# Fourier stage: widenings, filter products and returned blocks one part sooner; scan: SiLU block ahead of the decay of step 5

## What is computed

```python
x = x + _L0_conv_ref(_gn(x), ...)   # 3x3 neighbours weighted by a score
x = x + _L1_conv_ref(_gn(x), ...)   # two selective-scan (mamba) layers over the pixels
x = x + _L2_conv_ref(_gn(x), ...)   # Fourier filter on 8x8 patches, 3x3 conv, gated GELU
x = x + _L3_conv_ref(_gn(x), ...)   # cosine transform of 8x8 blocks, rounded
```

```python
dA = exp(delta * A); dBu = delta * B * u
h = dA[t] * h + dBu[t];  y[t] = sum_n h * C[t];  y = (y + u * D) * silu(res)
```

```python
x = einsum(x, w_in)                       # 64 -> 384 channels
x = irfft2(rfft2(8x8 patches of x) * fft_filter)
x = depthwise 3x3 conv of x;  x1, x2 = split(x)
return einsum(gelu(x1) * x2, w_out)       # 192 -> 64 channels
```

## Time and profile before

| | us |
|---|---|
| median of 3 runs | 19109.42 |
| lowest, highest | 19099.32, 19221.73 |
| the profiled execution, its own time | 19099.55 |
| its span, first to last instruction | 19097.7 |
| VectorE busy | 17998.3 (94%) |
| GpSimd busy | 17116.8 (90%) |
| TensorE busy | 13183.2 (69%) |
| ScalarE busy | 11214.6 (59%) |

### The profile page before, as it was taken

The page is one execution under the profiler, slowest core; times in us unless marked ns, Lnnn a source line. Parts: engine busy times, 40 slices in busy tenths (PEclk is TensorE's granted clock), DMA queues, the critical chain, the costliest instruction groups (busy, mean ns, idle before and its releaser), DMA issues. The chain is left out here.

```text
span 19097.7 us, 148278 instructions
## 1 busy us (share of the span) xinstructions
PE 13183.2 (69%) x46046; PEld 4686.6 (25%) x46046; DVE 17998.3 (94%) x11644; ACT 11214.6 (59%) x12335; POOL 17116.8 (90%) x7353
## 2 busy tenths in 40 slices
PE   4876666666666666666666666666666669999985
PEld 2321111111111111111111111111111134444444
DVE  5989999999999999999999999999999979999996
ACT  1116666666666666666666666666666646666663
POOL 3989999999999999999999999999999969999991
PEclk8997777777777777777777777777777779999997
DMA  4335555555555555555555555555555511111114
GB/s 125 114 109 138 134 135 139 139 134 138 139 134 136 140 138 133 137 139 137 134 139 139 134 137 140 137 133 138 139 138 134 137 49 34 34 34 34 34 29 146
DMA packets 616199, 2249.26 MB, mean 118 GB/s; under 512 B 74881, under 2 KB 92147, under 8 KB 591091
## 3 DMA queue, kind: packets, MB, share of 16 engines
q1 hardware_dynamic: 610146, 2232.63, 45.1%
q10 hardware_dynamic: 5265, 7.14, 0.1%
HBM read 990.77 MB, written 174.96 MB: 61 GB/s over the span
## 5 line engine op out<-in xcount | busy, mean ns | idle before, releaser
L1324 POOL TENSOR_TENSOR h<-h,c_bc 128x1024 f32<-128x1024 f32 x4096 | 9603.5, 2357 | 789.4 <-DVE h L1280 742.6
L1280 DVE TENSOR_TENSOR_SCAN h<-da,state,px 128x1024 f32<-128x1024 f32 x3072 | 7209.3, 2347 | 109.6
L1151 ACT ACTIVATE da<-d_bc,a_neg 128x1024 f32<-128x1024 f32 x3072 | 3492.6, 1144 | 2643.9 <-DVE h L1280 2619.4
L1005 PE MATMUL py<-h,ysel 128*32 128x512 f32 x16384 | 2740.3, 801 | 2587.8 <-POOL h L1324 2587.3
L1274 DVE TENSOR_TENSOR px<-px,du_bc 128x1024 f32<-128x1024 f32 x3072 | 3782.8, 1231 | 312.0 <-PE px L991 86.9
L1926 POOL TENSOR_TENSOR acc<-acc,ta 128x1024 f32<-128x1024 f32 (+1 forms) x976 | 2273.0, 2339 | 230.3 <-DVE acc L1826 135.8
L1316 POOL TENSOR_TENSOR xs<-du_bc,b_bc 128x1024 f32<-128x1024 f32 x1024 | 2409.6, 2353 | 0.0
L1280 DVE TENSOR_TENSOR_SCAN h<-px,state,xs 128x1024 f32<-128x1024 f32 x1024 | 2316.8, 2326 | 0.0
L1826 DVE SCALAR_TENSOR_TENSOR p_c<-zb,w_dw,p_c 128x1024 f32<-128x1024 f32 (+1 forms) x1560 | 1983.2, 1271 | 135.7 <-PE p_c L1591 112.2
L991 PE MATMUL px<-cf,bsel 32*128 32x512 f32 x3072 | 1339.8, 959 | 916.5 <-DVE h L1280 916.5
L1151 ACT ACTIVATE px<-d_bc,a_neg 128x1024 f32<-128x1024 f32 x1024 | 1144.6, 1118 | 900.6 <-DVE h L1280 885.9
(11 more groups left out here) (219 smaller groups left out, 19460.0 us busy)
## 6 DMA issues: line engine op xcount, KB each, us to landing
d_bc<-delta SPq DMA_DIRECT2D x1024, 512.0 KB, 8.5
du_bc<-du SPq DMA_DIRECT2D x1024, 512.0 KB, 8.5
c_bc<-c_rows_dram SPq DMA_DIRECT2D x1024, 512.0 KB, 5.3
b_bc<-c_rows_dram SPq DMA_DIRECT2D x256, 512.0 KB, 8.1
hx<-x_dram SPq DMA_DIRECT2D x252, 256.5 KB, 6.3
st_x<-in_x_dram SPq DMA_DIRECT2D x32, 1024.0 KB, 4.9
ax<-in_x_dram SPq DMA_DIRECT2D x64, 512.0 KB, 3.4
xr<-x_dram SPq DMA_DIRECT2D x64, 512.0 KB, 6.1
```

The source lines that it names most:

```text
L1005: last = nc.tensor.matmul(py[32 * j:32 * j + 32, cut], ysel[:, :], h[:, (4 * q + j) % 8, cut], start=False, stop=(q == Q - 1))
L1151: nc.scalar.activation(out[:, :], d_bc[:, n % J, :], ACT.Exp, scale=a_neg[t.l][:, n:n + 1]).then_inc(da_done, 1)
L1280: nc.vector.tensor_tensor_scan(h[:, n % 8, PAD:T + PAD], a[:, :], x[:, :], state[:, 2 * t.l + t.b, n:n + 1], ALU.mult, ALU.add).then_inc(s ...
L1324: nc.gpsimd.tensor_tensor(out=h[:, n % 8, 0:T], in0=h[:, n % 8, PAD:T + PAD], in1=c_bc[q % 2][:, :], op=ALU.mult).then_inc(m2_done, 1)
```

## The change

In the scan, ScalarE's `main` has the SiLU block of the task `after` ahead of decay 5 instead of behind it. In the Fourier stage the tables change: widening p moves from tick 3p + 1 to 3p, filter p from ahead of tap 3p + 3 to ahead of tap 3p + 2, the back-transforms by one tick; with them the pieces of unit 1 and one of unit 3 come a tick later, the next slot's first conv, the first projection, the third transpose and frequency step and GELU a tick sooner, and ScalarE's taps move by up to four ticks. No instruction is added or removed.

```diff
--- before.py
+++ after.py
@@ -1163,9 +1163,9 @@
                 decay(t, 4)
                 if before:
                     keep_state(before, 3)
-                decay(t, 5)
                 if after:
                     front_silu(after)
+                decay(t, 5)
                 decay(t, 6)
                 decay(t, 7)
                 if after:
@@ -1463,20 +1463,20 @@
         LOW, HIGH = slice(0, 64), slice(64, 128)
 
         TICKS = 6 * ND
-        CONV_AT = {0: (1, 0), 1: (1, 1), 5: (2, 0), 6: (2, 1), 7: (2, 2), 8: (2, 3), 10: (3, 0), 11: (3, 1),
+        CONV_AT = {1: (1, 0), 2: (1, 1), 5: (2, 0), 6: (2, 1), 7: (2, 2), 8: (2, 3), 10: (3, 0), 12: (3, 1),
                    15: (4, 0), 16: (4, 1), 17: (4, 2), 18: (4, 3), 20: (5, 0), 21: (5, 1), 22: (5, 2), 23: (5, 3)}
-        NEXT_AT = 27
-        PROJECT_AT = (4, 9)
-        WIDEN_AT = {3 * p + 1: p for p in range(NP)}
-        BACK_AT = {3 * (j // 2) + 4 + j % 2: j for j in range(NJ)}
+        NEXT_AT = 26
+        PROJECT_AT = (3, 9)
+        WIDEN_AT = {3 * p: p for p in range(NP)}
+        BACK_AT = {3 * (j // 2) + 3 + j % 2: j for j in range(NJ)}
 
         FIRST = 3
-        TURN_AT = ({13: 0, 19: 1, 25: 2}, {13: 3})
-        FREQ_AT = ({17: 0, 22: 1, 26: 2}, {16: 3})
-        TAP_AT = {2: (0, 0), 3: (0, 1), 4: (0, 2), 5: (1, 0), 6: (1, 1), 7: (1, 2), 9: (2, 0), 10: (2, 1), 14: (3, 0), 16: (3, 1),
-                  18: (3, 2), 21: (4, 0), 22: (4, 1), 26: (5, 0), 27: (5, 1)}
-        CARRY_AT, GELU_BACK_AT, GELU_AT = 1, (11, 12), (23, 24)
-        FILTER_N = {3 * p + 3: p for p in range(NP)}
+        TURN_AT = ({13: 0, 19: 1, 24: 2}, {13: 3})
+        FREQ_AT = ({17: 0, 22: 1, 25: 2}, {16: 3})
+        TAP_AT = {2: (0, 0), 3: (0, 1), 5: (0, 2), 6: (1, 0), 8: (1, 1), 9: (1, 2), 10: (2, 0), 13: (2, 1), 15: (3, 0), 16: (3, 1),
+                  18: (3, 2), 24: (4, 0), 26: (4, 1), 27: (5, 0), 28: (5, 1)}
+        CARRY_AT, GELU_BACK_AT, GELU_AT = 1, (11, 12), (22, 23)
+        FILTER_N = {3 * p + 2: p for p in range(NP)}
         RESIDUAL_N, STATS_N = (6, 12), (7, 13)
 
         @block.sync
```

## The result

The changed kernel takes 18968.9 us, median of 6 runs (18966.9 to 18971.7), against 19110.1 us for the kernel before in its 6 runs: a ratio of 0.9925, 95% interval 0.9914 to 0.9936. That is 141 us or 0.74% faster, 13 us under the forecast of 18982. Its profiled execution took 18966.9 us with a span of 18965.0, 132.7 us less than the span before.

The account below looks back on a forecast made before the run. VectorE was taken as the bound, its removable waits some 190 us. Scan 78 plus Fourier 44 make 122 us off the profiled 19099.55: 18977.5, plus half of the median's 9.9 us offset, 18982 us; range 18940 to 19075.

Parts of the forecast that it names:

- the Fourier term: Fourier stage: even slots, odd slots and ten lower-clock slots save 22 + 13 + 9 = 44 us; bounds -26 and 86.
- the lead-in: Stretch from last scan to first tap, ahead of the Fourier slots: forecast change 0 us.
- Scan: Scan stage: with SiLU one decay earlier, VectorE's 123 waits for px go, saving 78 us; bounds 0 and 87.
- (a): Start of a Fourier slot: filter 0 comes one tap sooner, so TensorE's list would start 1.32 us sooner.
- (b): Fourier slot, widening 5: TensorE waits 0.8 us for filter 4; last piece only 0.72 us sooner, even slots save 22 us.
- (c): VectorE in the Fourier stage: three more open gaps cost 0.42 us a slot; odd slots save 0.41 each, 13 us.
- (d): Ten Fourier slots with TensorE's clock low: its 0.8 us wait takes up half of 1.6 us each, 9 us saved.
- A: Fourier stage: filter 4 isn't late and TensorE keeps its whole lead, 27 us more saved, 18955 us; chance 0.18.
- B: Fourier stage gives nothing: the slot's tail or ScalarE's order eats the gain, 19026 us; chance 0.14.
- C: Scan gives nothing: another releaser, for instance the gate, stands behind L991, 19060 us; chance 0.08.
- D: Fourier stage: TensorE's waits at widenings 1 and 5 each bring a clock drop, 182 us lost, 19173 us; chance 0.04.
- The other moves of the tables: Fourier stage: GELU, ScalarE's taps, transposes, ft copies and block placing, each with cover, put at nothing.

Follow-up runs that it names:

- Experiment 7: The changed kernel with filter 4 one tap sooner still, ahead of tap 13 instead of 14: 18966.1 us (ratio 0.9929).
- experiment 4: The changed kernel with VectorE's filters back ahead of taps 3p + 3, all other tables new: 19120.9 us (ratio 1.0009).
- experiment 8: The changed kernel with filter 1 ahead of tap 4 (not 5) and filter 6 ahead of tap 21 (not 20): 18979.0 us (ratio 0.9935).
- Experiment 10: The changed kernel with filter 4 ahead of tap 13 and filter 1 ahead of tap 4, filter 6 where it was: 18954.1 us (ratio 0.9920).
- experiment 1: Each edit alone on the kernel before: the scan edit 19036.4 us (ratio 0.9962), the Fourier tables 19046.4 us (0.9968).
- experiment 5: The kernel before with only widening 0 moved to tick 0, ahead of unit 1's two pieces (ticks 1 and 2): 19171.2 us (ratio 1.0033).
- experiment 9: The changed kernel with filters ahead of taps 2, 4, 8, 11, 13, 17, 21, 23: 18955.9 us (ratio 0.9924).
- experiment 6: The kernel of experiment 4 with the slot's start as in the kernel before (unit 1 at ticks 0 and 1, widening 0 at tick 1): 19070.8 us (0.9992).

## Why the prediction was right

The mechanism was right in both stages. The time came out 13 us under the forecast because the Fourier term was 21 us too small and the lead-in, which I had put at nothing, took 9 us more; that these partly cancel is luck.

**Scan** (forecast 78, measured 74.3). Each step held: which wait, why it goes, ScalarE's wait for the gate taking its place, no loss at decay 5. The term was mis-sized by 4 us: I took 0.64 us net for a wait, the tasks show 54.73 - 54.13 = 0.60.

**Fourier (a) and (b)** (even slots forecast 48.90 - 0.72 = 48.18, measured 47.84). TensorE's list started 1.32 us sooner, as worked out, and it waited at widening 5, 1.05 us where I had 0.8. The last piece ended at the slot's start + 41.3, forecast + 41.65. The 0.3 us lie behind widening 5 (16.99 us from its start to the end of the last piece, where I had 17.31). I had taken the times between instructions from the old order; what shortened them no run shows. The sum for even slots was 22 us and came to 31 x 1.06 = 33. Experiment 7 shows that this wait was on the path, experiments 4 and 8 that a deadline beside it, unit 4's first tap, is nearly as tight; I had not named it.

**(c)** (forecast 0.42 us a slot). The gaps were priced about right, and the odd slot's wait was not. In the kernel before, first two taps at the border of two units without a wait, then the two around that wait:

```profile
17147.21 1.28 DVE L1826 SCALAR_TENSOR_TENSOR acc<-zb,w_dw,p_c 128x1024 f32<-128x1024 f32 x1
17148.41 3.93 DVE L1826 SCALAR_TENSOR_TENSOR p_c<-zb,w_dw,p_c 128x1024 f32<-128x1024 f32 x3
...
17187.49 1.27 DVE L1826 SCALAR_TENSOR_TENSOR acc<-zb,w_dw,p_c 128x1024 f32<-128x1024 f32 x1
17189.60 5.26 DVE L1826 SCALAR_TENSOR_TENSOR p_c<-zb,w_dw,p_c 128x1024 f32<-128x1024 f32 x4 [0.83 <-PE p_c L1591]
```

Where nothing is waited for, the first tap of a unit starts 1.20 us after the tap before, 0.08 us before that one ends. Around the wait they are 2.11 us apart. So the idle time in brackets, 0.83 us, understates the wait, which cost the slot 0.91. Odd slots rose from 47.68 - 0.91 = 46.77 without it to 47.17: 0.40 us for three gaps, 0.13 each. They saved 0.51 us a slot where I had 0.41, 31 x 0.51 = 16 us in place of 13. Experiment 10 gives 0.14 for one gap. By the Trainium skill (VectorE: DVE Perf Modes, "The DRAIN you can't avoid"), as the prediction reads it, these gaps would be zero, which is not borne out. The same section says that an instruction that is not held starts earlier, and that the traces show: an independent tap starts 1.20 us after one that takes 1.28.

**(d)** (forecast 9 us). All ten slots at the lower clock went, 10 x 1.58 = 16 us. I had counted on TensorE's wait absorbing half of their cost; what happened is that they did not occur, which I had no reason to expect: the 7 us more are luck. The Fourier term was too small by 11 us for the even slots, 7 here and 3 for the odd ones, 21 together. The +9 us of the lead-in, again the clock, hid part of it.

**Rivals.** A asked for even slots of 47.3 and a TensorE that does not wait at widening 5: it waits, and they are 47.84. B and C are refuted by the table of stretches and by experiment 1. D, the clock, was wrong here but is a real mechanism: experiment 5 is slower than the kernel before through it. I had looked for it in the added wait at widening 5, which did no harm, and not in the wait at widening 1, which the widening's move alone makes longer and the filter's move shortens again. The prediction also has ScalarE's taps up to three ticks later; it is up to four, and nothing in the result turns on it. The other moves of the tables, put at nothing, were not tried one by one; that the three items above add up to the 65 us fits with nothing.

## What to carry to other kernels

With two engines handing parts to and fro through single buffers, a table moved on one engine alone can lose more than the whole set gains: experiment 5 lost 66 us where the whole Fourier edit gains 63. Move producer and consumer together, and list every deadline of the new order, also that of work that the moved step now stands in front of. A wait is removed most cheaply where its holder is early for no use: ScalarE did a decay 13 us ahead of its reader while the chain behind SiLU was late. The idle time that a trace shows in front of an instruction can understate what the wait costs, since without the wait the instruction may overlap the one before; compare start to start. When a schedule changes an engine's waits, count the slots at the lower clock, before and after, as an item of its own.

## What the runs showed of the hardware

How often TensorE's clock fell changed with small changes of the order. In even slots TensorE waits at the slot's start, at widening 1 and at or behind widening 5. With waits of 1.5, 1.4 and 1.05 us (the changed kernel) and with 1.3, 1.4 and 0.2 (experiment 9) no slot was at the lower clock; with 1.9, 1.4 and 0.5 or 0.2 (experiments 7 and 10) six were; with one of 2.7 us (experiment 5) 32; with none over 2.2 (the profiled run of experiment 6) 43. These counts go by the output product. The record of the granted clock falls in more slots, 19, 15 and 59 in experiments 7, 10 and 6; some of these falls, early in the slot, cost nothing. What decides whether it falls is not shown. A slot at the lower clock cost 1.58 us in the kernel before, and up to 4 us in experiment 4, where it stayed low for longer. The lead-in of the Fourier stage took 121 to 137 us in the profiled runs, by the clock it got: a part of it takes 4.4 us at the higher level and 6.6 at the lower. And a VectorE tap of 1.28 us that reads what the tap before it wrote starts 1.32 us after it, one that does not 1.20; an independent instruction between them fills that gap, for 0.13 to 0.14 us a gap.
